# Linear attention stage: normalising on ScalarE, gates on GpSimd, shorter rank digits and softmax sum, and another order of the rounds

## The chip, the cores and the metric

One core of a Trainium2 chip runs the whole program. The time is that of one execution on the device in microseconds; three executions of the kernel before took 1861.42, 1862.78 and 1866.75 us (median 1862.78).

## The reference, cut to what matters

Sixteen sequences of 512 tokens of width 128 pass two layers. The change lies in the first: linear attention, a layer norm, and the routing of the mixture of experts that follows, with its shared expert.

```python
qkv = x @ W; q, k, v = split(qkv, 3)
q = elu(q) + 1; k = elu(k) + 1
KV = einsum('bld,blh->bhd', k, v); k_sum = k.sum(axis=1)
Z = 1 / (einsum('bld,bd->bl', q, k_sum) + 1e-6)
x = layernorm(x + einsum('bld,bhd,bl->blh', q, KV, Z))
probs = softmax(x @ gate_w.T)                # 32 experts
topk_w, topk_idx = top_k(probs, 4); topk_w /= sum(topk_w)
# the tokens of each expert in order of their number, 128 at most
# expert_out by its two matrices, gated, added; plus the shared expert
x = layernorm(x + routed + shared)
...
# second layer: state-space scan, layer norm, 8 experts with 2 of them, layer norm
```

## The kernel before, in words

Five engines run their own instruction lists and meet at semaphores: TensorE (PE) multiplies, VectorE (DVE), ScalarE (ACT) and GpSimd (POOL) compute, SyncE (SP) issues most DMAs. Up to about 270 us the program is in the first stage. It goes over the 16 sequences, one as a tile of 128 partitions by 4 times 128 columns. A sequence passes several steps, and each engine has a function `stage1` that in one round does the steps of several sequences in a fixed order: a is the newest sequence, r the one before it, l and p the two before that. TensorE's and VectorE's loops take two rounds in one turn; `at(per, k)` is the value of a semaphore that counts `per` to a sequence.

For sequence a: TensorE projects x to keys, values (kv, line 1091) and queries (q, line 1094). ScalarE takes the exponential, the copy of the values and the positive part (lines 863 to 870). VectorE adds them to kf and qf (lines 1467, 1475). TensorE makes the state kva (line 1125), ScalarE evicts it (kvx, line 885), TensorE multiplies by the queries (o, line 1131), VectorE divides and adds x (pre, line 1514) and takes the statistics. GpSimd makes 1/sqrt (rstd, lines 674, 676), and VectorE normalises (line 1452) into xg, whose last 32 columns take the gates.

For sequence r: TensorE transposes xg (line 1100), ScalarE evicts it (x1T, line 874), TensorE multiplies by the gate matrix and the shared expert's first matrices in one (line 1118). VectorE takes the eight largest logits of a row (top), subtracts the largest (lsub), finds the four chosen (mask, line 1500); ScalarE takes the exponential (lexp). VectorE multiplies both (gm, line 1509), sums (gs), inverts (gr) and writes the gates to xg (line 1529). The shared expert goes over hsh, its transpose (line 1137), its eviction (hshT, line 896) and the down product (line 1143) to resid. TensorE counts ranks from mask (lines 1147 to 1154), VectorE adds the carry of earlier sequences (rnk) and splits the rank into two digits by rounding with a large constant (rkt, rka, rkb, lines 1544 to 1551).

For sequence l: GpSimd subtracts the digits from all their values (dgb, dga, line 658), VectorE compares with zero (ohb, oha), ScalarE multiplies ohb by row and tile numbers (ohv, lines 889, 900). For sequence p: TensorE multiplies oha and ohv to a part of the experts' token lists (line 1110), and VectorE adds it to lsum (line 1471).

One order matters most: `need` is a wait until a tile has been read by its last user. So ohv of sequence l waits for the list product of the sequence before it, and TensorE's next projection writes into the memory that held o, so it waits for pre.

After the last round lsum is turned into indices (270 to 281 us), and the experts' tokens are gathered. SP's queue loads x two sequences ahead, and for each sequence stores a zero block, resid and xg, in that order, with a wait ahead of the last two.

## Time and profile before

| what | value |
| --- | --- |
| median of three runs | 1862.78 us |
| the profiled execution | 1860.44 us |
| its span, first to last instruction | 1858.8 us |
| mean granted TensorE clock over the span | 0.878 |
| TensorE, VectorE, ScalarE, GpSimd busy | 78%, 76%, 53%, 75% of the span |
| the first stage, to the end of the last lsum | 270.5 us |

The profiled execution is 1.6 us longer than its span, and 2.3 us shorter than the median. A row of the timeline has start, length, engine, line, operation, output and inputs with their shapes, and how many instructions were merged; in square brackets stands how long the engine was idle before it and what released it. A granted clock of 1.00 is 2.4 GHz, 0.50 is 1.2 GHz.

### The profile page before, as it was taken

What the parts mean: (1) busy time and instruction counts of PE and PEld (TensorE: products, weight loads), DVE (VectorE), ACT (ScalarE), POOL (GpSimd) and SP (SyncE); (2) the same over time, 40 slices, a digit from 0 to 9 for tenths busy, and PEclk for the clock granted to TensorE, in tenths of its full rate; (3) what the DMA queues carried; (4) which work ended last, traced back from release to release, by engine and by line L of the source; (5) the groups of instructions that cost most, each with busy time, mean ns of one, the idle gap of its engine ahead of it and who ended that gap; (6) DMA issues with size and microseconds to landing.
All of it is one profiled execution on the core that took longest, in us unless ns stands there. A gap on an engine that the chain in (4) does not pass through costs nothing.

```text
span 1858.8 us, 23733 instructions
## 1 busy us (share of the span) xinstructions
PE 1442.2 (78%) x5979; PEld 865.5 (47%) x6020; DVE 1407.2 (76%) x2764; ACT 977.2 (53%) x1676; POOL 1385.6 (75%) x962
## 2 busy tenths in 40 slices
PE   5777753425998889988899889988884989939881
PEld 3665642322443334433344334433342758938771
DVE  3898941112999999999999999999995576528884
ACT  2454520103655666556665566556642558827670
POOL 2554465753999999999999999999981455577785
PEclk8899965557999999999999899998997999969995
...
GB/s 149 110 89 89 103 161 218 63 45 128 68 105 91 126 131 75 93 96 129 131 58 85 120 131 103 75 88 163 120 7 127 36 65 129 149 82 158 149 147 81
DMA packets 201422, 198.62 MB, mean 107 GB/s; under 512 B 22664, under 2 KB 180296, under 8 KB 197064
## 3 DMA queue, kind: packets, MB, share of 16 engines
...
## 4 chain that ended last, share of the span: by engine, by line
PE 30%; DVE 21%; issue 15%; POOL 11%; DMA 6%; ACT 2%; DVEq 1%; POOLq 0%; SPq 0%; another core or an unknown queue 0%; ACTq 0%
PE bank L1272 12%; DVE hst L1646 11%; PE bank L1227 5%; POOL sorted_rows L828 3%; DMA sorted_rows<-x3b,row_of 2%; POOL yg L840 2%; DVE prod L1662 2%; POOL dbx L778 2%; PE bank L1261 1%; PE bank L1285 1%; PE bank L1225 1%; DVE st L1443 1%; PE bank L1239 1%; POOL xe L712 1%; DMA yg<-expert_rows,row_of 1%
## 5 line engine op out<-in xcount | busy, mean ns | idle before, releaser
L778 POOL TENSOR_TENSOR dbx<-u,ball 128x1024 f32<-128x1024 f32 x256 | 614.2, 2500 | 5.7 <-POOL u L809 2.8
L1646 DVE TENSOR_TENSOR_SCAN hst<-bank,dbx 128x512 f32<-128x512 f32 x512 | 592.3, 1207 | 8.6 <-POOL dbx L778 4.1
L1272 PE MATMUL bank<-prod,ident 128*128 128x512 f32 x1024 | 514.2, 639 | 20.1 <-DVE prod L1662 14.8
L983 ACT ACTIVATE bank<-dt,aneg 128x511 f32<-128x511 f32 x512 | 346.9, 689 | 276.9 <-DVE hst L1646 275.1
L1272 PEld LDWEIGHTS bank<-prod,ident 128*128 128x128 f32 x1024 | 207.1, 205 | 261.1 <-issue 210.8
L1662 DVE TENSOR_TENSOR prod<-hst,bank 128x1024 f32<-128x1024 f32 x192 | 233.7, 1217 | 17.2 <-DVE hst L1646 13.8
L787 POOL TENSOR_TENSOR prod<-hst,call 128x1024 f32<-128x1024 f32 x64 | 161.1, 2517 | 22.5 <-DVE hst L1646 22.3
L840 POOL DMA_INDIRECT yg<-expert_rows,row_of x128 | 128.6, 1005 | 47.2 <-issue 37.8
L1256 PE MATMUL bank<-parts,sel_c 128*128 128x512 bf16 x152 | 60.8, 401 | 73.6 <-DVE prod L1662 72.9
L828 POOL DMA_INDIRECT sorted_rows<-x3b,row_of x80 | 78.9, 986 | 51.6 <-DMA sorted_rows<-x3b,row_of 32.4
L1227 PE MATMUL bank<-x2T,inc 128*128 128x512 f32 x256 | 117.0, 600 | 0.0
L828 POOL DMA_INDIRECT sorted_rows<-x3a,row_of x48 | 46.8, 975 | 64.2 <-DMA sorted_rows<-x3a,row_of 36.5
L1365 PE MATMUL bank<-xu,wv 128*128 128x256 f32 x192 | 51.5, 391 | 42.1 <-DVE hg L1685 42.1
L1388 PE MATMUL bank<-wv,hg 128*128 128x128 f32 x384 | 77.0, 283 | 4.9 <-ACT yu L1058 4.9
L1256 PEld LDWEIGHTS bank<-parts,sel_c 128*128 128x128 bf16 x192 | 18.8, 98 | 132.3 <-DVE prod L1662 88.3
L1227 PEld LDWEIGHTS bank<-x2T,inc 128*128 128x128 f32 x256 | 49.4, 193 | 63.1 <-issue 63.1
L1052 ACT ACTIVATE hg<-hg 128x512 f32<-128x512 f32 x64 | 40.4, 632 | 67.8 <-DVE hg L1685 66.9
L1685 DVE SCALAR_TENSOR_TENSOR hg<-bank,wv,ha 128x256 f32<-128x256 f32 x96 | 42.0, 480 | 44.4 <-ACT ha L1036 44.0
L1389 PE MATMUL bank<-wv,hgb 128*128 128x128 f32 x384 | 75.5, 279 | 0.0
L1388 PEld LDWEIGHTS bank<-wv,hg 128*128 128x128 f32 x384 | 62.3, 196 | 12.0 <-ACT yu L1058 10.1
L658 POOL TENSOR_TENSOR dga<-rka,iota_e 128x2048 bf16<-128x2048 f32 x16 | 58.7, 3669 | 11.9 <-DVE ohb L1480 11.2
L658 POOL TENSOR_TENSOR dgb<-rkb,iota_e 128x1024 bf16<-128x1024 f32 x16 | 31.3, 1955 | 48.2 <-DVE rkb L1551 48.2
...
## 6 DMA issues: line engine op xcount, KB each, us to landing
...
```

Of the source, the lines that this page charges most:

```text
L658: gp.tensor_tensor(dst[:, :, :], a, b, ALU.subtract).then_inc(done, 1)
L778: gp.tensor_tensor(dbx[n % NDB][:, :, :], u[s.par][:, :, :], ball[:, n:n + 1, :].to_broadcast([P, NH, SEQ]), ALU.mult).then_inc(dbx_rdy, 1)
L787: gp.tensor_tensor(prod[2][:, :, :], hst[2][:, :, :], call[:, k:k + 1, :].to_broadcast([P, NH, SEQ]), ALU.mult).then_inc(pprod_rdy, 1)
L828: gp.indirect_dma_start(xs_d[b][:, :], bass.IndirectOffsetOnAxis(row_of[:, c, k:k + 1], 0), x3_tile(k), None).then_inc(sent[b], 16)
L840: gp.indirect_dma_start(yg[q % 3][:, k, c, :], None, y_d[b][:, :], bass.IndirectOffsetOnAxis(row_of[:, c, q * TT + k:q * TT + k + 1], 0)). ...
L983: act.activation(da_ps[h][:, 1:SEQ], dt_[s.par][:, h, 1:SEQ], ACT.Exp, scale=aneg[:, h, n:n + 1]).then_inc(da_rdy, 1)
L1227: last = mm(pb_ps[:, :], inc[:, k, tile(h)], x2T[:, k:k + SEQ], start=False, stop=(k == DCONV - 1))
L1256: mm(cb_ps[k % 2][:, :], sel_c[:, n, :], parts[s.par][:, :], start=True, stop=True).then_inc(cb_rdy, 1)
L1272: last = mm(y_ps[:, h, :], ident[:, :], from_[:, h, :], start=False, stop=(n == NS - 1), skip_group_check=True)
L1388: mm(yu_ps[:, tile(k)], hg[g % 2][:, tile(k)], w[:, W2A:W2B], start=True, stop=False)
L1646: dve.tensor_tensor_scan(h_of[:, h, :], da_ps[h][:, :], dbx[n % NDB][:, h, :], 0.0, ALU.mult, ALU.add).then_inc(scan_rdy, 1)
L1662: tt(prod[k % 2][:, :, :], h_of[:, :, :], over_h(cb_ps[k % 2]), ALU.mult).then_inc(prod_rdy, 1)
```

## The change

Five things change in the first stage; the rest of the program is as before, except that two semaphores are shared and so counted on.

- ScalarE normalises (one `activation` with scale rstd and bias -mean x rstd, four times a sequence). GpSimd makes the bias with two small instructions more.
- GpSimd multiplies lexp by mask and by gr and writes the gates.
- The sum of the softmax is that of the four largest: VectorE subtracts in `top` (tsub), ScalarE takes the exponential (texp), and the sum goes over four columns.
- The rank is split by one rounding with another constant (rka, rkb). The digits' values lie in two small tables.
- A round has six sequences: n (the next to be projected), a, r, l, p and o, whose lists are added. TensorE projects n, and ScalarE evicts it, in the middle of the round of a. All engines and SP's queue have another order. VectorE does resid for l, one round later than before, and lsum for o, also a round later. SP stores the gates ahead of resid, and loads x one sequence further ahead.

The diff, cut to the orders and the moved work (the bookkeeping lines `settle` and blank lines are left out without a mark):

```diff
...
+MAGIC_8 = 100663296.0
+MIDDLE = SLOT_B / 2 - 0.5
...
+def rounds(eng, stage, last):
+    q = lambda b: Seq(0, b) if 0 <= b < NB else None
+    for i in range(4):
+        stage(q(i), q(i - 1), q(i - 2), q(i - 3), q(i - 4), q(i + 1))
+    with eng.bass.Fori(0, NB // 2 - 3, engines=(eng.engine,), hint_back_edge=True) as j:
+        for i in (4, 5):
+            stage(*[Seq(j, i - k) for k in range(5)], Seq(j, i + 1))
+    for i in range(NB - 2, last):
+        stage(q(i), q(i - 1), q(i - 2), q(i - 3), q(i - 4), q(i + 1))
...
             def store_routed(s):
                 sp.dma_start(r2_d[bass.ds(s.at(SEQ), SEQ), :].rearrange("(t p) d -> p t d", p=P),
                              zero[:, 0:D].rearrange("p (t d) -> p t d", t=1).to_broadcast([P, TT, D])).then_inc(zeros_stored, 16)
+                sp.wait_ge(x1_rdy, s.at(TT, TT))
+                sp.wait_ge(gates_rdy, s.at(2, 2))
+                sp.dma_start(xg_d[bass.ds(s.at(SEQ), SEQ), :].rearrange("(t p) d -> p t d", p=P), xg[s.par][:, :, :]
+                             ).then_inc(st_xg[s.par], 16)
                 sp.wait_ge(resid_rdy, s.at(1, 1))
                 sp.dma_start(r_d[bass.ds(s.at(SEQ), SEQ), :].rearrange("(t p) d -> p t d", p=P), resid[:, :, :]
                              ).then_inc(st_r, 16)
-                sp.wait_ge(route0, s.at(15, 15))
-                sp.dma_start(xg_d[bass.ds(s.at(SEQ), SEQ), :].rearrange("(t p) d -> p t d", p=P), xg[s.par][:, :, :]
-                             ).then_inc(st_xg[s.par], 16)
...
+            def root_and_shift(s):
+                gp.wait_ge(mv_rdy, s.at(8, 8))
+                need(gp, x1_rdy, s.at(TT))
+                gp.tensor_scalar(rstd[:, :], mv[:, :, 1], LN_EPS, None, ALU.add).then_inc(rstd_rdy, 1)
+                gp.tensor_scalar(nmean[:, :], mv[:, :, 0], -1.0, None, ALU.mult).then_inc(rstd_rdy, 1)
+                gp.wait_ge(rstd_rdy, s.at(4, 2))
+                gp.tensor_tensor(rstd[:, :], rstd[:, :], neghalf[:, :], ALU.pow).then_inc(rstd_rdy, 1)
+                gp.wait_ge(rstd_rdy, s.at(4, 3))
+                gp.tensor_tensor(nmean[:, :], nmean[:, :], rstd[:, :], ALU.mult).then_inc(rstd_rdy, 1)
+            def gates_of(s):
+                gp.wait_ge(route0, s.at(14, 12))
+                gp.wait_ge(lexp_rdy, s.at(1, 1))
+                gp.tensor_tensor(gm[:, :, :], lexp[:, :, :], mask[:, :, :], ALU.mult).then_inc(gates_rdy, 1)
+                gp.wait_ge(gates_rdy, s.at(2, 1))
+                gp.wait_ge(route0, s.at(14, 14))
+                need(gp, st_xg[s.par], s.half(16))
+                gp.tensor_tensor(xg[s.par][:, :, D:XGW], gm[:, :, :], gr[:, :].rearrange("p (t e) -> p t e", e=1).to_broadcast([P, TT, E0]),
+                                 ALU.mult).then_inc(gates_rdy, 1)
...
+            def stage1(a, r, l, p, o, n):
+                if l:
+                    slots_of(l)
+                if a:
+                    root_and_shift(a)
+                if r:
+                    gates_of(r)
+            rounds(gp, stage1, NB + 2)
...
+            def stage1(a, r, l, p, o, n):
                 if a:
+                    act.wait_ge(kva_mm, a.at(1, 1))
+                    need(act, o_mm, a.at(1))
+                    act.activation(kvx[:, :], kva_ps[:, 0:D + 1], ACT.Copy).then_inc(kvx_rdy, 1)
                 if r:
                     act.wait_ge(t_mm, r.at(1, 1))
                     need(act, gu_mm, r.at(1))
                     act.activation(x1T[:, :], t_ps[:, :], ACT.Copy).then_inc(x1T_rdy, 1)
                     act.wait_ge(gu_mm, r.at(1, 1))
+                    need(act, route0, r.at(14))
                     act.activation(lg[:, :, :], gu_ps[:, :, 0:E0], ACT.Copy
                                    ).then_inc(lg_rdy, 1)
                     need(act, sg_rdy, r.at(1))
                     act.activation(tg[:, :, :], gu_ps[:, :, E0:E0 + I0], ACT.Tanh).then_inc(tg_rdy, 1)
                 if l:
                     act.wait_ge(ohb_rdy, l.at(1, 1))
                     need(act, list_mm, l.at(1))
                     act.activation(ohv[0][:, :, :, :], ohb[:, :, :, :], ACT.Identity, scale=row_no[:, 0:1]).then_inc(ohv_rdy, 1)
                     for k in range(TT):
                         act.activation(ohv[1][:, k, :, :], ohb[:, k, :, :], ACT.Identity, scale=tile_no[:, bass.ds(l.at(TT, k), 1)]
                                        ).then_inc(ohv_rdy, 1)
+                if r:
+                    act.wait_ge(route0, r.at(14, 6))
+                    need(act, gates_rdy, r.at(2))
+                    act.activation(texp[:, :, :], tsub[:, :, :], ACT.Exp).then_inc(texp_rdy, 1)
+                    act.activation(lexp[:, :, :], lsub[:, :, :], ACT.Exp).then_inc(lexp_rdy, 1)
+                if n:
+                    keys(n)
+                if r:
+                    act.wait_ge(hshT_mm, r.at(1, 1))
+                    need(act, d_mm, r.at(1))
+                    act.activation(hshT[:, :], t_ps[0:I0, :], ACT.Copy).then_inc(hshT_rdy, 1)
+                if n:
+                    queries(n)
+                if a:
+                    act.wait_ge(rstd_rdy, a.at(4, 4))
+                    need(act, st_xg[a.par], a.half(16))
+                    need(act, t_mm, a.at(1, -1))
+                    need(act, resid_rdy, a.at(1, -1))
+                    for k in range(TT):
+                        act.activation(xg[a.par][:, k, 0:D], pre[:, k, :], ACT.Identity, bias=nmean[:, k:k + 1], scale=rstd[:, k:k + 1]
+                                       ).then_inc(x1_rdy, 1)
...
+            def project(n):
+                pe.wait_ge(ldx[n.par], n.half(32, 32))
+                need(pe, pre_rdy, n.at(TT))
...
+                last.then_inc(kv_mm, 1)
+                need(pe, qf_rdy, n.at(1))
+                mm(q_ps[:, :], wt["Wq"][:, :], xT[n.par][:, :], start=True, stop=True).then_inc(q_mm, 1)
+            def stage1(a, r, l, p, o, n):
                 if a:
+                    pe.wait_ge(kf_rdy, a.at(1, 1))
+                    pe.wait_ge(v_rdy, a.at(1, 1))
+                    need(pe, list_sum, a.at(1, -3))
...
+                    last.then_inc(kva_mm, 1)
                 if r:
                     pe.wait_ge(x1_rdy, r.at(TT, TT))
                     need(pe, hshT_rdy, r.at(1))
+                    need(pe, rank0, r.at(4, -2))
...
                     last.then_inc(t_mm, 1)
+                if a:
+                    pe.wait_ge(kvx_rdy, a.at(1, 1))
+                    pe.wait_ge(qf_rdy, a.at(1, 1))
...
+                    last.then_inc(o_mm, 1)
+                if r:
+                    pe.wait_ge(x1T_rdy, r.at(1, 1))
+                    need(pe, lg_rdy, r.at(1))
+                    need(pe, hsh_rdy, r.at(1))
...
+                    last.then_inc(gu_mm, 1)
                 if p:
                     pe.wait_ge(ohv_rdy, p.at(5, 5))
                     pe.wait_ge(oha_rdy, p.at(1, 1))
+                    need(pe, list_sum, p.at(1))
...
                     last.then_inc(list_mm, 1)
+                if n:
+                    project(n)
                 if r:
                     pe.wait_ge(hsh_rdy, r.at(1, 1))
...
                     last.then_inc(hshT_mm, 1)
                     pe.wait_ge(hshT_rdy, r.at(1, 1))
                     need(pe, resid_rdy, r.at(1))
...
                     last.then_inc(d_mm, 1)
+                    pe.wait_ge(route0, r.at(14, 12))
...
+            def stage1(a, r, l, p, o, n):
+                if o:
+                    dve.wait_ge(list_mm, o.at(1, 1))
...
+                    tt(lsum[:, :], lsum[:, :], list_ps, ALU.add).then_inc(list_sum, 1)
                 if a:
                     dve.wait_ge(ek_rdy, a.at(1, 1))
...
                     stt(kf[:, :, :], ek[:, :, :], 1.0, kv_ps[:, :, 0:D], ALU.min, ALU.add).then_inc(kf_rdy, 1)
                     dve.wait_ge(eq_rdy, a.at(1, 1))
...
                     stt(qf[:, :], eq[:, :], 1.0, q_ps[:, :], ALU.min, ALU.add).then_inc(qf_rdy, 1)
                 if l:
+                    dve.wait_ge(d_mm, l.at(1, 1))
...
+                    tt(resid[:, :, :], blk4(d_ps), xg[l.par][:, :, 0:D], ALU.add).then_inc(resid_rdy, 1)
+                if a:
+                    dve.wait_ge(o_mm, a.at(1, 1))
+                    ts(den[:, :], o_ps[:, :, D], Z_EPS, None, ALU.add).then_inc(rz_rdy, 1)
...
+                    dve.reciprocal(rz[:, :], den[:, :]).then_inc(rz_rdy, 1)
+                if l:
                     dve.wait_ge(dg_rdy, l.at(2, 1))
...
                     ts(ohb[:, :, :, :].rearrange("p t e b -> p (t e) b"), dgb[:, :, :], 0.0, None, ALU.is_equal).then_inc(ohb_rdy, 1)
+                if a:
...
+                    dve.wait_ge(ldx[a.par], a.half(32, 32))
...
+                    for k in range(TT):
+                        stt(pre[:, k, :], o_ps[:, k, 0:D], rz[:, k:k + 1], xt[a.par][:, k, :], ALU.mult, ALU.add
+                            ).then_inc(pre_rdy, 1)
+                    dve.wait_ge(pre_rdy, a.at(TT, TT))
...
+                    stats_of(pre, stats, mv, a, mv_rdy)
                 if r:
                     dve.wait_ge(lg_rdy, r.at(1, 1))
...
                     dve.wait_ge(tg_rdy, r.at(1, 1))
...
                     tt(lsub[:, :, :], gu_ps[:, :, 0:E0], top[:, :, 0:1].to_broadcast([P, TT, E0]), ALU.subtract).then_inc(route0, 1)
...
+                    tt(tsub[:, :, :], top[:, :, 0:TOPK], top[:, :, 0:1].to_broadcast([P, TT, TOPK]), ALU.subtract).then_inc(route0, 1)
...
                     stt(sg[:, :, :], tg[:, :, :], 1.0, gu_ps[:, :, E0:E0 + I0], ALU.add, ALU.mult).then_inc(sg_rdy, 1)
                     dve.wait_ge(sg_rdy, r.at(1, 1))
...
                     tt(hsh[:, :, :], sg[:, :, :], gu_ps[:, :, E0 + I0:GW], ALU.mult).then_inc(hsh_rdy, 1)
...
                     tt(mask[:, :, :], rep[:, :, :], lg[:, :, :], ALU.not_equal).then_inc(route0, 1)
+                    dve.wait_ge(texp_rdy, r.at(1, 1))
+                    dve.tensor_reduce(gs[:, :], texp[:, :, :], AX.X, ALU.add).then_inc(route0, 1)
...
+                    dve.reciprocal(gr[:, :], gs[:, :]).then_inc(route0, 1)
                 if l:
                     dve.wait_ge(dg_rdy, l.at(2, 2))
...
                     ts(oha[:, :, :, :].rearrange("p t e a -> p (t e) a"), dga[:, :, :], 0.0, None, ALU.is_equal).then_inc(oha_rdy, 1)
                 if r:
                     dve.wait_ge(mt_mm, r.at(1, 1))
                     tt(rnk[:, :].rearrange("p (t e) -> p t e", t=TT), rank_ps.rearrange("p (t e) -> p t e", t=TT),
                        carry[:, :].rearrange("p (t e) -> p t e", t=1).to_broadcast([P, TT, E0]), ALU.add).then_inc(rank0, 1)
...
                     tt(carry[:, :], carry[:, :], tot_ps, ALU.add).then_inc(rank0, 1)
...
+                    ts(rka[:, :], rnk[:, :], MAGIC_8, MAGIC_8, ALU.add, ALU.subtract).then_inc(rank0, 1)
...
+                    tt(rkb[:, :], rnk[:, :], rka[:, :], ALU.subtract).then_inc(rank0, 1)
+            rounds(dve, stage1, NB + 4)
...
```

## Rows read from the trace of the kernel before

**Rows 1.** Busy time by stretch: length, each engine's busy us, granted clock, DMA share

```profile
60.39:231.64 171.25, 132.75 (x1135) 106.48 (x1131) 152.31 (x613) 88.86 (x193) 85.59 (x48) 0.91 0.33 96
231.64:270.46 38.82, 19.06 (x204) 17.32 (x200) 20.42 (x87) 12.09 (x27) 23.98 (x21) 0.63 0.47 137
```

**Rows 2.** Timeline, VectorE: kf of five sequences, the last lsum (start us, length us)

```profile
33.36 0.69 DVE L1467 SCALAR_TENSOR_TENSOR kf<-ek,bank 128x512 f32<-128x512 f32 x1 [8.90 <-ACT bank L866]
...
60.39 0.69 DVE L1467 SCALAR_TENSOR_TENSOR kf<-ek,bank 128x512 f32<-128x512 f32 x1
...
203.50 0.69 DVE L1467 SCALAR_TENSOR_TENSOR kf<-ek,bank 128x512 f32<-128x512 f32 x1 [0.33 <-issue]
...
217.37 0.68 DVE L1467 SCALAR_TENSOR_TENSOR kf<-ek,bank 128x512 f32<-128x512 f32 x1
...
231.64 0.69 DVE L1467 SCALAR_TENSOR_TENSOR kf<-ek,bank 128x512 f32<-128x512 f32 x1
...
270.04 0.42 DVE L1471 TENSOR_TENSOR lsum<-lsum,bank 128x256 f32<-128x256 f32 x1 [5.27 <-issue]
```

**Rows 3.** Instructions by line, VectorE, 100 to 214 us (busy us, mean ns)

```profile
L1452 DVE TENSOR_SCALAR xg<-pre,mv,rstd 128x128 f32<-128x128 f32 x32 | 8.9, 344 | 0.1
...
L1529 DVE TENSOR_TENSOR xg<-gm,gr 128x128 f32<-128x128 f32 x8 | 2.3, 291 | 0.3
...
L1546 DVE TENSOR_SCALAR rkt<-rkt 128x128 f32<-128x128 f32 x8 | 1.8, 227 | 0.3
```

**Rows 4.** Timeline: mask without and with GpSimd's dga; GpSimd's power

```profile
39.21 0.29 DVE L1500 TENSOR_TENSOR mask<-rep,lg 128x128 bf16<-128x128 f32 x1
...
120.63 3.67 POOL L658 TENSOR_TENSOR dga<-rka,iota_e 128x2048 bf16<-128x2048 f32 x1 [0.74 <-DVE ohb L1480]
...
122.76 1.68 DVE L1500 TENSOR_TENSOR mask<-rep,lg 128x128 bf16<-128x128 f32 x1
...
128.25 1.04 POOL L676 TENSOR_TENSOR rstd<-rstd,neghalf 128x4 f32<-128x4 f32 x1
```

**Rows 5.** Timeline, TensorE, one round at granted clock 1.00

```profile
217.08 1.10 PE L1110 MATMUL bank<-ohv,oha 128*128 128x64 bf16 x32
218.32 1.35 PE L1118 MATMUL bank<-wcat,x1T 128*128 128x160 f32 x8
219.51 1.06 PE L1125 MATMUL bank<-vext,kf 128*128 128x129 f32 x8
220.94 1.16 PE L1131 MATMUL bank<-kvx,qf 128*128 128x129 f32 x8 [0.37 <-ACT kvx L885]
...
223.25 1.16 PE L1143 MATMUL bank<-w_sd,hshT 64*128 64x128 f32 x8 [0.68 <-ACT hshT L896]
...
224.62 0.25 PE L1154 MATMUL bank<-mask,onesb 128*128 128x32 bf16 x4
```

**Rows 6.** Timeline, ScalarE: evictions, ohv and, from the second layer, x3o

```profile
115.35 0.60 ACT L863 ACTIVATE ek<-bank 128x512 f32<-128x512 f32 x1 [4.70 <-PE bank L1091]
...
116.84 0.60 ACT L869 ACTIVATE eq<-bank 128x512 f32<-128x512 f32 x1
...
120.95 1.14 ACT L889 ACTIVATE ohv<-ohb,row_no 128x1024 bf16<-128x1024 bf16 x1
...
122.86 0.59 ACT L896 ACTIVATE hshT<-bank 64x512 f32<-64x512 f32 x1 [0.57 <-PE bank L1137]
...
123.36 1.70 ACT L900 ACTIVATE ohv<-ohb,tile_no 128x256 bf16<-128x256 bf16 x4
...
541.74 1.50 ACT L1007 ACTIVATE x3o<-bank,nm,rs 128x128 f32<-128x128 f32 x4
```

**Rows 7.** Busy time of a stretch at low granted clock (columns as in rows 1)

```profile
47.50:50.50 3.00, 3.00 (x14) 2.83 (x12) 1.47 (x9) 0.55 (x2) 2.36 (x2) 0.50 0.73 230
```

**Rows 8.** Timeline, TensorE: kva in that stretch; a projection behind a wait

```profile
48.71 1.93 PE L1125 MATMUL bank<-vext,kf 128*128 128x129 f32 x8
...
111.83 3.48 PE L1091 MATMUL bank<-w_Wkv,xT 128*128 128x256 f32 x8 [1.08 <-DVE pre L1514]
```

252 lines of the change are left out of this document (80 added, 172 removed).

## The prediction

> **What bounds the kernel now.** I read the busy table by stretch first, then the timeline of two rounds, then durations by line, and last the rows where TensorE's granted clock is low. The change touches only the first stage (linear attention and its router, from the start to about 270 us of the 1858.8 us span); what follows starts from the finished lists and moves with their end. The stage works in rounds, one sequence entering per round. In the twelve rounds between the second and the last kf shown [rows 1, 2], 60.39 to 231.64 us, a round takes 171.25 / 12 = 14.27 us, and VectorE is busy for 152.31 / 12 = 12.7 us of it, TensorE 11.1, ScalarE 7.4, GpSimd 7.1. So VectorE bounds the round. The rounds shown whole take 13.87 us (203.50 to 217.37) and 14.27 us (to 231.64) [rows 2]. The last sequence then needs 38.8 us more, from its kf to the end of the last lsum [rows 1, 2].
>
> **What VectorE loses.** Per round go: the four normalising instructions (8.9 us in eight rounds, 1.11 each round), the two gate products (0.29 each), and two of the four steps that split the rank (0.23 each) [rows 3]: 2.1 us. The softmax sum over four columns instead of 32 gives at most 0.1 and needs a small subtraction more, bounded by 0 and by a product's 0.29; I take 0.2. A larger gain is hidden: mask takes 0.29 us where GpSimd is idle, and 1.68 us where GpSimd's dga runs; it starts at 122.76 and ends at 124.44, just after dga (120.63 + 3.67 = 124.30) [rows 4]. In the new order dga starts earlier against mask and is over by then, so 1.4 us more go. VectorE keeps 12.7 - 2.1 + 0.1 - 1.4 = 9.3 us of work a round. If it still bounded the round, 3.4 us would go from each.
>
> **What the new order chains together.** That gain is not on the path any more, because in the new order one chain goes through all engines once a round. I follow it from the start of kf at 0, with durations at the full clock. On TensorE the order is now kva, transpose of x1, o, gate/up product, list product, projection of the next sequence, hsh transpose, down product, ranks. kf ends at 0.69 and kva starts at 0.75 (1.06 long). The old gap from kva's start to o's start is 220.94 - 219.51 = 1.43 us and holds ScalarE's eviction; the transpose now sits in it and makes it about 1.5, so o starts at 2.3. o (1.16), gate/up (1.35) and list (1.10), less the 0.1 to 0.16 by which neighbours overlap (gate/up starts at 218.32 and kva at 219.51), end at 5.6 [rows 5]. ScalarE's ohv of sequence l may only overwrite its tile when the list product of sequence l-1 has read it; that product was early in the round and is now behind gate/up, so ohv starts at 5.7. The two steps of ohv take 1.14 + 1.70, 2.64 with their overlap, and the two exponentials behind them 0.3 (an estimate from the ratio of sizes to the 0.60 rows): 8.6. Only then come the three evictions of the next projection (115.35 to 116.84: 1.49), at 10.1, and the hsh eviction (0.59), at 10.7 [rows 6]. The down product waits for that and ranks stand behind it: 223.25 to 224.87, 1.62 us [rows 5], so 12.4. On VectorE the rank sum, carry, the two digits and the lsum of the next round, five instructions of 0.2 to 0.4 us [rows 2, 3], add 1.4 before the next kf. The sum is 13.8 us a round at the full clock, about what the shorter of the two rounds shown takes now. The projection itself (pre ends at 5.3, list at 5.6; by columns at kva's rate it is an estimated 3.1 us, so until 8.7) stands beside ohv, and the queries' two evictions and the normalising stand behind hsh's eviction, beside the down product.
>
> **Moved work costed at nothing, and its cover.** Normalising on ScalarE is like four of x3o, 1.50 us [rows 6]; it ends near 13.2, and the transpose that reads it comes at 15.3 in this count, so 2 us of cover; beyond that TensorE is held one for one. The gate products on GpSimd lie between dga / 16 = 0.23 us by size and the 0.6 of a full eviction; I take 0.5 each, since a fixed part must be there. GpSimd then carries dga (3.67), dgb (half of it, 1.8), the power (1.04), three small steps that I bound together by another 1.04, and the products, 8.6 us of 13.8 [rows 4]; its last product ends near 11.2 and the next digits come at 13.1. The stores and loads on SP's queue number the same; the gate store now goes ahead of the residual store and waits for a product of the round before, and the load of the next x stands in front of it: one round of cover each, cost 0, bounds 0 and 0.4 us a round.
>
> **The clock.** Between 47.5 and 50.5 us the granted clock was 0.50 (1.2 GHz) [rows 7], and kva took 1.93 us instead of 1.06 [rows 5, 8]. The projection at 111.83, after TensorE had waited 1.08 us for pre, took 3.48 us [rows 8]. Over the twelve rounds the clock averages 0.91 [rows 1], so TensorE is at the lower level for 18% of the time; today it can fall on the projection, as at 111.83, which has VectorE's work of 12.7 us a round beside it. In the new order TensorE waits twice: 1.5 us between hsh's transpose (an estimated 0.6 behind the projection, so 9.3) and the down product (10.8), and 2.1 us between the ranks (12.4) and the next kva (14.5), with 1.6 us of work between. The low stretches should therefore fall on kva, o, gate/up and list, which are all on the path. I price it so: the low share can hardly be under today's 18% of some 14.5 us, 2.6 us a round, of which five sixths meet TensorE work on the path and lose half: 1.1 us. With twice that share it is 2.2; with none it is 0. I take 1.1, since the waits are longer than today's but the work between is the same. A round is then 13.8 + 1.1 = 14.9 us.
>
> **The sum.** Twelve rounds: 12 x (14.9 - 14.27) = +7.6 us. The two rounds before them (33.36 to 60.39 [rows 2]) lack ohv or lists in either order: 0, bounds -1 and +1. The tail gains since VectorE's freed work and mask stand on its chain, but its clock is low for long (0.63 [rows 1]): -1.5 us, bounds -3 and 0. Together +6.1 us. The profiled execution took 1860.4 us, so 1866.5; the median of the runs, 1862.8, lies 2.3 above it, so I say **1869 us**.
>
> **Rivals.**
> First, **the clock holds** and the round is 13.8 us: 12 x (13.8 - 14.27) - 1.5 to -3 = -7.1 to -8.6 us, so 1855 us. The place is TensorE's wait between ranks and kva. It ends on the other side where low stretches cost under 0.6 us a round (13.8 + 0.6 = 14.4, and 12 x 0.13 pays for the tail). For it: TensorE's work from kva to the projection is now one unbroken stretch. Against it: the two long waits.
> Second, **both cancel**: low stretches in about half of the rounds, 14.1 to 14.7 us a round, which is -3.5 to +3.7 us: 1863.
> Third, **low in twice the share**: 2.2 us, a round of 16.0, 12 x 1.73 - 1.5 = +19 us: 1882. TensorE has then fallen to 1.2 GHz at the waits of every round, and recovers only behind gate/up. The Trainium skill (TensorE: Matmul & The Clock Gate, "What's actually happening") calls the throttled state the default that activity releases; by that rule the new waits bring this case, and the row at 111.83 agrees with its direction, though not every wait of today is followed by a low clock.
> Fourth, **VectorE's time is the round's time** after all, that is, the chain above is looser than I read it: 12 x -3.4 = -41 us, 1822. Against it: every link is an order on one engine or a tile that must be free.
>
> **How the numbers follow.** About 0.3% (5.6 us) is what a measurement of this kernel can tell from no change. The forecast has 0.36 (its own range 1866 to 1875), of which 0.04 would still measure within the bound, the third rival 0.07: slower 0.39. Both cancelling has 0.31, with those 0.04: same 0.35. The clock holding has 0.23 and the fourth 0.03: faster 0.26. The range from 1853 to 1880 leaves out the fourth, the far half of the third and the ends of the unknown costs.
>
> **What would show it.** In the changed kernel's profile kf should follow kf by 14.4 to 15.4 us; VectorE should wait for o (near 1.3 us) and, before the rank sum, for TensorE (near 0.5 to 1.5 us), and its busy time in the stage should fall by some 50 us without the stage ending earlier. Mask should take 0.3 to 0.5 us. ScalarE should run from the gate logits to hsh's eviction with hardly a gap, and ohv should start on the list product's end. Low-clock stretches should begin near the ranks and cover kva and o. I am wrong if kf follows kf by under 14 us, if the down product does not wait for ScalarE, or if the clock stays full at the start of the rounds.

## The result, and the profile after

The changed kernel takes **1891.79 us** (median of 4 runs, 1886.23 to 1893.11) against 1864.49 us (4 runs of the kernel before, on the same chip): a ratio of **1.0142, 95% interval 1.0115 to 1.0168**. It is slower by 27 us. Forecast were 1869 us and a range of 1853 to 1880: the sign is the forecast's, the size is not.

First, busy time by stretch in the changed kernel, with the columns of [rows 1] (length; busy us and count of TensorE, its weight loads, VectorE, ScalarE and GpSimd; granted clock, DMA share, GB/s): the twelve rounds from kf of the fourth sequence to kf of the last, the tail behind them, and two neighbouring stretches inside the rounds.

```profile
62.51:260.02 197.51, 146.98 (x1128) 127.97 (x1128) 120.97 (x529) 107.95 (x252) 102.30 (x97) 0.76 0.27 82
260.02:298.50 38.48, 21.82 (x216) 19.62 (x216) 19.47 (x78) 14.25 (x33) 23.78 (x26) 0.63 0.35 100
107.91:118.15 10.24, 7.71 (x45) 7.38 (x44) 4.01 (x12) 3.03 (x8) 2.16 (x2) 0.50 0.19 58
118.15:124.98 6.83, 5.00 (x52) 3.69 (x51) 6.12 (x33) 5.76 (x14) 6.15 (x6) 1.00 0.36 115
```

A round takes 197.51 / 12 = **16.46 us** where it took 14.27. VectorE is busy for 120.97 / 12 = 10.1 us of it, where it was 12.7, so it no longer bounds anything. The granted clock averages 0.76 where it was 0.91. In the middle of the stage three fifths of a round run at 1.2 GHz: 10.24 us at 0.50, then 6.83 us at 1.00.

The same rounds on VectorE's timeline (rows as in [rows 2]):

```profile
34.95 0.69 DVE L1519 SCALAR_TENSOR_TENSOR kf<-ek,bank 128x512 f32<-128x512 f32 x1 [13.10 <-ACT bank L916]
...
62.51 0.68 DVE L1519 SCALAR_TENSOR_TENSOR kf<-ek,bank 128x512 f32<-128x512 f32 x1
...
128.66 0.68 DVE L1519 SCALAR_TENSOR_TENSOR kf<-ek,bank 128x512 f32<-128x512 f32 x1
...
260.02 0.68 DVE L1519 SCALAR_TENSOR_TENSOR kf<-ek,bank 128x512 f32<-128x512 f32 x1
...
298.08 0.42 DVE L1515 TENSOR_TENSOR lsum<-lsum,bank 128x256 f32<-128x256 f32 x1 [2.05 <-PE bank L1194]
```

The stage ends at 298.50 us, 28.0 later than before (270.46). Of that, 1.6 us are there at the second kf (34.95 against 33.36), 0.5 come in the next two rounds (27.56 us against 27.03), 12 x 2.19 = 26.3 in the twelve rounds, and the tail gives 0.3 back (38.48 against 38.82). What follows the stage took 4.7 us more in this execution (1891.5 - 298.5 = 1593.0 against 1588.3). Its code is nearly the same; in the fifteen experiments below it took 1591 to 1601, so I read nothing from it.

One round of the chain, from the timeline of all engines:

```profile
112.52 2.08 PE L1164 MATMUL bank<-vext,kf 128*128 128x129 f32 x8 [2.53 <-DVE kf L1519]
...
115.25 1.93 PE L1177 MATMUL bank<-kvx,qf 128*128 128x129 f32 x8
...
116.97 1.83 PE L1184 MATMUL bank<-wcat,x1T 128*128 128x160 f32 x8
...
118.21 3.67 POOL L683 TENSOR_TENSOR dga<-rka,iota_a 128x2048 bf16<-128x2048 f32 x1 [4.99 <-DVE ohb L1535]
...
118.64 1.10 PE L1194 MATMUL bank<-ohv,oha 128*128 128x64 bf16 x32
...
119.77 1.15 ACT L942 ACTIVATE ohv<-ohb,row_no 128x1024 bf16<-128x1024 bf16 x1 [0.29 <-PE bank L1194]
...
121.11 0.81 DVE L1556 TENSOR_TENSOR tsub<-top 128x16 f32<-128x16 f32 x1
...
122.73 0.57 ACT L913 ACTIVATE ek<-bank 128x512 f32<-128x512 f32 x1
...
124.20 0.58 ACT L958 ACTIVATE hshT<-bank 64x512 f32<-64x512 f32 x1
...
124.83 1.97 PE L1208 MATMUL bank<-w_sd,hshT 64*128 64x128 f32 x8 [1.38 <-ACT hshT L958]
...
127.13 0.27 PE L1219 MATMUL bank<-mask,onesb 128*128 128x32 bf16 x4
...
127.44 0.29 DVE L1580 TENSOR_TENSOR rnk<-bank,carry 128x128 f32<-128x128 f32 x1 [2.76 <-PE bank L1219]
...
128.66 0.68 DVE L1519 SCALAR_TENSOR_TENSOR kf<-ek,bank 128x512 f32<-128x512 f32 x1
...
129.40 1.87 PE L1164 MATMUL bank<-vext,kf 128*128 128x129 f32 x7 [2.00 <-DVE kf L1519]
```

(The last row counts only the products inside the window.) Every link of the predicted chain is there, in its order: ohv starts 0.03 us after the list product's end, the keys' evictions and hsh's eviction stand behind it on ScalarE, the down product waits for the latter, the ranks stand behind that, and kva waits 2 us for kf. What differs is TensorE's own part: down, kva, o and gate/up take 1.97, 2.08, 1.93 and 1.83 us here, and took 1.16, 1.06, 1.16 and 1.35 in [rows 5].

Instructions by line from 62.51 to 260.02 us, answering to [rows 3, 4] (us busy, mean ns, idle us in front in all twelve rounds):

```profile
L967 ACT ACTIVATE xg<-pre,nmean,rstd 128x128 f32<-128x128 f32 x48 | 19.7, 490 | 0.0
...
L1208 PE MATMUL bank<-w_sd,hshT 64*128 64x128 f32 x96 | 17.9, 342 | 15.5 <-ACT hshT L958 15.5
...
L1556 DVE TENSOR_TENSOR tsub<-top 128x16 f32<-128x16 f32 x12 | 10.0, 835 | 0.0
L713 POOL TENSOR_TENSOR gm<-lexp,mask 128x128 f32<-128x128 f32 x12 | 9.1, 755 | 0.7
...
L718 POOL TENSOR_TENSOR xg<-gm,gr 128x128 f32<-128x128 f32 x12 | 4.8, 401 | 3.7 <-POOL gm L713 3.7
...
L1569 DVE TENSOR_TENSOR mask<-rep,lg 128x128 bf16<-128x128 f32 x12 | 3.5, 292 | 1.3
...
L1529 DVE TENSOR_SCALAR den<-bank 128x4 f32<-128x4 f32 x12 | 1.9, 162 | 42.3 <-PE bank L1177 42.3
```

The mask takes 0.29 us in every round, as said. VectorE waits 42.3 / 12 = 3.5 us a round for o. GpSimd's exclusion has moved to tsub, which has 16 elements a partition and takes 0.84 us.

### The profile page after: what moved, and what is told of

Its sections match the earlier page's. It is cut to its first block, busy times and chain, and to the rows that moved or that the text cites. A ratio compares the mean times of both kernels' runs of the same rounds, so it can differ in the third digit from the quotient of the medians.

```text
span 1891.5 us, 23767 instructions
## 1 busy us (share of the span) xinstructions
PE 1458.5 (77%) x5979; PEld 890.3 (47%) x6020; DVE 1368.0 (72%) x2652; ACT 1001.0 (53%) x1756; POOL 1406.8 (74%) x1028
## 4 chain that ended last, share of the span: by engine, by line
PE 28%; DVE 19%; issue 15%; POOL 12%; DMA 8%; ACT 1%; DVEq 1%; POOLq 0%; SPq 0%; another core or an unknown queue 0%; ACTq 0%
PE bank L1329 13%; DVE hst L1673 11%; PE bank L1284 5%; POOL sorted_rows L879 5%; POOL yg L891 3%; DMA sorted_rows<-x3a,row_of 3%; DMA sorted_rows<-x3b,row_of 2%; DVE prod L1689 2%; PE bank L1318 1%; PE bank L1282 1%; PE bank L1342 1%; PE bank L1296 1%; DVE st L1500 1%; POOL dbx L829 1%; DVE y L1659 1%
## 5 line engine op out<-in xcount | busy, mean ns | idle before, releaser
L1689 DVE TENSOR_TENSOR prod<-hst,bank 128x1024 f32<-128x1024 f32 x192 | 233.4, 1216 | 17.2 <-DVE hst L1673 13.8
L683 POOL TENSOR_TENSOR dga<-rka,iota_a 128x2048 bf16<-128x2048 f32 x16 | 58.7, 3672 | 64.3 <-issue 36.1
L771 POOL DMA_INDIRECT resid_rows<-ye,ixs x32 | 50.8, 1587 | 19.3 <-issue 13.6
```

What stands on the lines that cost most here:

```text
L1689: tt(prod[k % 2][:, :, :], h_of[:, :, :], over_h(cb_ps[k % 2]), ALU.mult).then_inc(prod_rdy, 1)
```

## Experiments

The ratios are to the kernel before, measured on the same chip as each kernel; the changed kernel's own is 1.0142. "A round" is the mean of the twelve from the fourth kf to the last in the profile.

### Is it the clock? Three kernels with TensorE kept at work

The edit of **e1_fill**: small products of constants into the gate/up bank, in both waits. Behind hsh nobody reads that bank until the next gate/up product.

```diff
+            def fill(n):
+                for k in range(n):
+                    mm(gu_ps[:, k % TT, 0:P], onesb[:, :], upper[:, :], start=True, stop=True)
...
                     last.then_inc(hshT_mm, 1)
+                    fill(20)
                     pe.wait_ge(hshT_rdy, r.at(1, 1))
...
                     last.then_inc(mt_mm, 1)
+                    fill(28)
```

> The changed kernel with TensorE kept at work in its two long waits: 20 small bf16 products (128 columns, 0.055 us each at the full clock by the ranks' rows) ahead of the down product, 28 behind the ranks, into the gate/up bank, which nobody reads by then; no output changes. Theory, the clock: the chain alone is 13.8 us a round and the low clock makes it 16.5, so with the clock held kf should follow kf by 13.8 to 14.4 us and the time fall by 12 x 2.1 to 2.7 = 25 to 32 us, to 1860 to 1867. Rival, the chain is longer than summed and the low clock only falls into time that is waited anyway: kf to kf stays above 16 and the time above 1885; where the fillers delay kva and the down product, it is slower than the changed kernel by up to 12 x 1.5 = 18 us.

Measured: 1865.7 us, ratio 0.9990 [0.9966, 1.0014]: the whole loss is gone. Busy time of its twelve rounds, and TensorE's timeline at the start of one:

```profile
60.14:228.42 168.28, 148.44 (x1714) 128.16 (x1712) 121.01 (x529) 108.66 (x252) 102.39 (x97) 1.00 0.32 97
```

```profile
159.01 1.15 PE L1168 MATMUL bank<-vext,kf 128*128 128x129 f32 x8 [0.90 <-DVE kf L1525]
...
160.62 1.16 PE L1181 MATMUL bank<-kvx,qf 128*128 128x129 f32 x8
161.61 1.25 PE L1188 MATMUL bank<-wcat,x1T 128*128 128x160 f32 x8
...
169.11 1.16 PE L1213 MATMUL bank<-w_sd,hshT 64*128 64x128 f32 x8
```

The clock is 1.00 through all twelve rounds, and a round takes 168.28 / 12 = 14.02 us. VectorE, ScalarE and GpSimd are as busy as in the changed kernel to within 1 us; nothing but the clock and the 576 fillers is different. So the low clock costs 16.46 - 14.02 = **2.44 us a round**, 29 us in the stretch.

**e11_fill_down** keeps the first `fill(20)` alone.

> The changed kernel with the 20 fillers ahead of the down product alone, and none behind the ranks. If the wait ahead of the down product is what lets the clock fall, the round is e1_fill's 14.0 us and the time 1863 to 1869. If it is the wait between the ranks and kva, the round stays at 16 us or more, 1883 to 1892. If both do, half comes back: 14.6 to 15.6 us, 1872 to 1883.

Measured: 1872.3 us, ratio 1.0043 [1.0024, 1.0062], a round 180.07 / 12 = 15.01 us, clock 0.92. Both waits count: filling the one ahead of the down product brings back 1.45 us of the 2.44, and filling the one between the ranks and kva as well brings the other 1.0. The second wait was not filled alone.

```profile
59.03:239.10 180.07, 140.77 (x1368) 122.17 (x1368) 121.04 (x530) 108.25 (x252) 102.38 (x97) 0.92 0.30 91
```

**e8_before_fill** puts 10 and 16 fillers at the same places into the kernel *before*.

> The kernel before with filling products at the same two places, 10 ahead of the down product and 16 behind the ranks. Theory: there the low clock (0.91 on average) falls mostly beside VectorE's 12.7 us of work a round and costs little: 0 to 0.4 us a round back, 1858 to 1866 where the kernel before has 1863 to 1867. Rival: the low clock costs the old order as well, 0.18 x 14.27 / 2 = 1.3 us a round: 1847 to 1851. Rival, slower: the fillers delay the next projection, up to 12 x 0.9 us, 1876.

Measured: 1874.15 us, ratio 1.0028 [1.0013, 1.0042], which is 8 us above the range that the theory gave.

```profile
60.40:232.14 171.74, 139.51 (x1431) 117.66 (x1427) 152.56 (x613) 88.86 (x192) 85.57 (x48) 0.97 0.33 96
```

The rounds have the clock at 0.97 instead of 0.91 and take 171.74 / 12 = 14.31 us, against 14.27, and VectorE is as busy in them as before (152.56 us against 152.31). What the run loses lies behind them, 2.4 us of it in the tail (41.2 us against 38.8). So with two thirds of its low time gone the old order's round was no shorter: its low stretches lay beside VectorE's work. That is why the same clock could be overlooked there and not here.

### Is the chain the chain? One link shortened at a time

**e4_ranks_first** puts the ranks ahead of the down product, both behind hsh's eviction.

```diff
                     pe.wait_ge(hshT_rdy, r.at(1, 1))
-                    need(pe, resid_rdy, r.at(1))
...
-                    last.then_inc(d_mm, 1)
                     pe.wait_ge(route0, r.at(14, 12))
...
                     last.then_inc(mt_mm, 1)
+                    need(pe, resid_rdy, r.at(1))
...
+                    last.then_inc(d_mm, 1)
```

> The changed kernel with the ranks ahead of the down product on TensorE (both still behind ScalarE's eviction of hsh). Theory, one chain: the down product, 1.97 us at the low and 1.16 at the full clock, leaves the way to the rank sum and kf and lies beside VectorE's five small steps: 1.2 to 2.0 us off each of 12 rounds, 14 to 24 us, to 1868 to 1878. Rival, the clock sets the period: 1886 to 1892, with kf to kf near 17 us from 94 to 180 us. Rival, slower: the shorter wait in front of kva moves nothing and resid, later now, holds VectorE: above 1892.

Measured: 1872.32 us, ratio 1.0038 [1.0024, 1.0052], a round 178.14 / 12 = 14.84 us: 1.6 us off, the middle of what was expected.

```profile
59.55:237.69 178.14, 142.29 (x1129) 123.17 (x1128) 121.06 (x529) 108.50 (x254) 102.33 (x97) 0.81 0.30 92
```

The down product was on the path to kf because the ranks stood behind it. But the 1.6 us are not the link's alone: the clock rose from 0.76 to 0.81, which is 38% of 14.84 us or 5.6 us at the low level against 7.9, and at the 2.44 / 7.9 = 0.31 us that such a microsecond cost in the changed kernel that is an estimated 0.7 us.

**e3_ohb_early** puts ohb ahead of VectorE's wait for o.

```diff
                     tt(resid[:, :, :], blk4(d_ps), xg[l.par][:, :, 0:D], ALU.add).then_inc(resid_rdy, 1)
+                if l:
+                    dve.wait_ge(dg_rdy, l.at(2, 1))
+                    need(dve, ohv_rdy, l.at(5))
+                    ts(ohb[:, :, :, :].rearrange("p t e b -> p (t e) b"), dgb[:, :, :], 0.0, None, ALU.is_equal).then_inc(ohb_rdy, 1)
                 if a:
                     dve.wait_ge(o_mm, a.at(1, 1))
```

> The changed kernel with ohb (its digits are ready at 113.2) put ahead of the wait for o on VectorE, where that engine stands idle for 3.6 us. GpSimd's dga then ends before tsub. Theory, one chain: ohb's 0.43 us leaves the way from o to hsh, and tsub, 0.81 us now because it ends only with dga, shrinks to about 0.2: 1.0 us off each round, 12 to 13 us, to about 1879; TensorE's wait before the down product shrinks by at most the 0.6 us until ScalarE's ohv ends, and if ohv and the keys behind it hold that wait, only 0 to 0.5 us of each round is gained: 1886 to 1892. Rival, moved operations are what costs (the lock between GpSimd and VectorE): the gain is larger than 1.0 us a round, below 1875.

Measured: 1885.54 us, ratio 1.0101 [1.0073, 1.0130], a round 15.62 us: 0.8 us less, where 1.0 was expected, or at most 0.5 if ohv and the keys hold the wait.

```profile
63.16:250.60 187.44, 136.92 (x1128) 118.49 (x1128) 113.78 (x530) 107.52 (x252) 104.37 (x97) 0.82 0.28 86
```

```profile
L1208 PE MATMUL bank<-w_sd,hshT 64*128 64x128 f32 x96 | 13.9, 285 | 22.0 <-ACT hshT L958 22.0
```

ohv and the keys do hold it: the down product waits 22.0 us for ScalarE in the twelve rounds, and 15.5 in the changed kernel. What shortened the round is mostly the clock again, 0.82 against 0.76: by the estimate given for e4_ranks_first 0.7 of the 0.8 us. So ohb and tsub were hardly on the chain.

**e2_kf_first** makes kf and qf a function of their own, `features`, and calls it for the next sequence ahead of the rank sum.

```diff
+                if n:
+                    features(n)
                 if r:
                     dve.wait_ge(mt_mm, r.at(1, 1))
```

> The changed kernel with the next sequence's kf and qf put ahead of the rank sum on VectorE. Theory, one chain: rank sum, carry, two digits and lsum stand between the ranks and kf, from 127.44 to 128.66 us in the profile of the changed kernel, and kva starts 2.0 us after the ranks end; kf's input is there 3 us before. With kf ahead, kva follows the ranks at once: 2.0 us off each of some 13 rounds, 26 us, to about 1866, and more (to 1855) where the shorter wait also lifts the clock. Rival, VectorE's later work or the normalising is as late: kva then waits in front of the transposes and under 6 us are gained. Rival, the clock alone sets it: the period stays near 17 us in the stretch from 94 to 180 us and nothing is gained there.

Measured: 1884.91 us, ratio 1.0120 [1.0084, 1.0156], far above the 1866 expected. The next run shows the miss best. **e5_fill_kf** is e2_kf_first with 24 fillers ahead of the down product.

> The changed kernel with kf and qf ahead of the rank sum (as in e2_kf_first) and 24 filling products ahead of the down product; none behind the ranks, since that wait is gone with kf there. Theory, a chain whose length the clock sets: e2_kf_first ran its two rounds at the full clock in 11.94 and 11.99 us (43.50 to 67.43) and then, with low stretches, 15.5 on average; with the clock held all rounds should take 12.0 to 12.5: 12 x 2 us less than e1_fill's 14.02, that is 1840 to 1848, and below the kernel before. Rival, one filled wait is not enough: low stretches stay in every second round or more, 13.5 to 15 us a round, 1858 to 1876.

Measured: 1863.77 us, ratio 0.9975 [0.9961, 0.9990], a round 14.0 us, clock 0.96: in the range of the rival, and not the 1840 to 1848 expected. Rounds at the full clock take 13.3 to 13.8 us there. One row of its TensorE timeline tells what I had left out:

```profile
99.39 0.82 PE L1168 MATMUL bank<-vext,kf 128*128 128x129 f32 x5 [1.85 <-DVE lsum L1528]
```

kva (whose last products lie outside the window) waits 1.85 us, and no longer for kf but for lsum. kva and the list lie in one PSUM bank, and the kernel has kva wait until VectorE has added the list (`need(pe, list_sum, ...)`); lsum still stood behind the ranks. The two rounds of 12 us at the full clock, from which I took the expectation, had no list sum yet. A wait has two ends to move, and I moved one.

### The chain made shorter

**e6_list_early** joins e5_fill_kf and e3_ohb_early and moves the list product to the start of the round, ahead of kva, with its sum behind ScalarE's eviction of kva. **e10_no_fill** is the same without fillers.

```diff
             def stage1(a, r, l, p, o, n):
+                if p:
+                    pe.wait_ge(ohv_rdy, p.at(5, 5))
...
+                    last.then_inc(list_mm, 1)
                 if a:
                     pe.wait_ge(kf_rdy, a.at(1, 1))
...
-                if o:
-                    dve.wait_ge(list_mm, o.at(1, 1))
+                if p:
+                    dve.wait_ge(list_mm, p.at(1, 1))
+                    dve.wait_ge(kvx_rdy, a.at(1, 1) if a else NB)
```

> e5_fill_kf with two more steps taken off the chain: ohb ahead of the wait for o on VectorE (e3_ohb_early), and the list product moved from behind gate/up to the start of the round, ahead of kva, with the list sum behind ScalarE's eviction of kva. Theory: the list product's 1.1 us is on the chain at either place, but ScalarE's ohv may then start behind the tanh, 0.4 us earlier, and lsum's 0.42 leaves the chain, so 11.2 to 12.0 us a round: 1830 to 1842. Rival: the list product ahead of kva delays kva by its whole 1.1 us and ohv is held by something else: 12.5 to 13 us a round, 1846 to 1854. Rival, the clock falls in the longer wait between projection and hsh's transpose: above 1856.

Measured: 1847.29 us, ratio **0.9894** [0.9877, 0.9910], a round 149.27 / 12 = 12.44 us at clock 1.00. That is near the first rival's figures, and faster than both kernels.

> e6_list_early without any filling products. Theory, the wait ahead of the down product alone lets the clock fall: low stretches in most rounds, 13.5 to 15.5 us a round, 1860 to 1885. Rival, with the list product moved into the other wait TensorE stays busy enough: no or few low stretches, 12.1 to 12.6 us, 1844 to 1851. This tells whether the fillers or the shorter chain hold the clock in e6_list_early.

Measured: 1844.03 us, ratio 0.9898 [0.9874, 0.9923]. The rival was right. Its twelve rounds, and the seven of them between 105.83 and 190.11:

```profile
53.76:205.21 151.45, 121.66 (x1128) 99.84 (x1128) 115.24 (x530) 106.90 (x253) 103.75 (x97) 0.95 0.35 106
105.83:190.11 84.28, 67.52 (x659) 54.68 (x660) 66.66 (x310) 62.91 (x149) 60.54 (x57) 1.00 0.38 114
```

Those seven take 84.28 / 7 = 12.04 us each, at the full clock and without fillers. With the list product in the wait between ranks and kva these rounds need no filler. The waits in them are shorter than those of the changed kernel too (at most 1.2 us on TensorE from 118 to 145 us, against 2.5 in the row at 112.52), and which of the two holds the clock was not separated.

**e9_best** takes three more things off the chain: the list sum goes behind oha, hsh's eviction goes ahead of two of the keys' evictions, and there are 14 fillers instead of 24. **e13_short_chain** drops the fillers and puts rank sum, carry and digits between kf and qf.

```diff
                 if n:
-                    keys(n)
+                    keys_exp(n)
                 if r:
...
                     act.activation(hshT[:, :], t_ps[0:I0, :], ACT.Copy).then_inc(hshT_rdy, 1)
                 if n:
+                    keys(n)
+                if n:
                     queries(n)
```

> e6_list_early with three more steps: the list sum behind the one-hot oha and no longer between o and the row sums (0.41 us), ScalarE's eviction of hsh behind the first of the keys' three evictions and no longer behind all (hsh's transposes end at 165.75, the eviction starts at 166.15: 0.4 us), and 14 fillers in place of 24 (24 of them ended 0.3 us after the eviction). Theory, one chain at the full clock: 12.3 - 1.0 = 11.2 to 11.6 us a round, 8 to 13 us less than e6_list_early: 1834 to 1840. Rival, 14 fillers don't hold the clock: low stretches come back, 1847 or more. Rival, something else is next (the keys' evictions in front of kf, or GpSimd's dga in front of tsub): 12.0 us, 1842 to 1847.

Measured: 1838.89 us, ratio **0.9861** [0.9842, 0.9880], but 148.46 / 12 = 12.37 us a round, no shorter than e6_list_early. The stage ends 2.0 us earlier (244.8 us against 246.9); the rest of the 8 us between the medians lies behind it, and the intervals of the two ratios overlap. The next bound was one row away: ohb now waits for the digits, `[1.68 <-POOL dgb L683]`, and den, which could start at o's end (160.61), starts at 161.60.

> e9_best without fillers (e10_no_fill held the full clock without them in nine rounds) and with the rank sum, carry and the two digits between kf and qf on VectorE. In e9_best the digits were ready only at 158.97, so ohb waited 1.68 us for GpSimd's dgb and den started 1.0 us after o's end. Theory, that wait is the chain's: digits 1.0 us earlier, den on o's end: 12.4 - 0.7 to 1.0 = 11.4 to 11.7 us a round, 8 to 12 us less than e9_best: 1827 to 1832. Rival, qf, now 0.7 us later, holds o: 12.0 to 12.4 us, 1836 to 1842. Rival, without fillers the clock falls in some rounds, as in three of e10_no_fill's: +1 us in each, 1832 to 1845.

Measured: 1840.32 us, ratio 0.9867 [0.9845, 0.9890]: the same as e9_best. Five of its rounds:

```profile
129.35:186.66 57.31, 48.54 (x472) 39.30 (x471) 48.09 (x221) 44.75 (x106) 42.50 (x40) 1.00 0.39 120
```

57.31 / 5 = 11.46 us, as the chain said. But single rounds of 12.96 and 16.41 us with low stretches bring the mean of twelve to 12.03, and what the stage still gains (its end is at 240.1 us against 244.8) does not show in the medians.

### Order or operations? The changed operations in the old order

**e7_old_order** keeps before's order on every engine and has the four changed operations in it. On GpSimd and at the end of ScalarE's round, against the kernel before:

```diff
+            def stage1(a, r):
+                if a:
+                    root_and_shift(a)
+                if r:
+                    gates_of(r)
+                    slots_of(r)
...
+                if a:
+                    act.wait_ge(rstd_rdy, a.at(4, 4))
...
+                        act.activation(xg[a.par][:, k, 0:D], pre[:, k, :], ACT.Identity, bias=nmean[:, k:k + 1], scale=rstd[:, k:k + 1]
+                                       ).then_inc(x1_rdy, 1)
```

> The order of the kernel before on all engines, with the changed operations in it: normalising on ScalarE at the end of its round, both gate products on GpSimd ahead of the digits, the rank digits by one rounding, the softmax sum from the four maxima. Theory, the new order is what costs: VectorE, which bounds the old order, loses 2.1 us of work a round and the time falls by 12 x 1 to 2.1 us or more, to 1837 to 1853. Rival, the moved operations cost (GpSimd's products and root, ScalarE's normalising as late as before's): the round does not shorten, or lengthens; 1860 to 1892. By e1_fill the rival is the less likely.

Measured: 1910.1 us, ratio 1.0221 [1.0204, 1.0238], a round 16.87 us: slower than the changed kernel, and above the range of the rival too. Four rows of its timeline:

```profile
196.58 3.63 PE L1140 MATMUL bank<-w_Wkv,xT 128*128 128x256 f32 x8
...
199.63 1.65 ACT L949 ACTIVATE xg<-pre,nmean,rstd 128x128 f32<-128x128 f32 x4 [4.01 <-POOL nmean L691]
...
202.85 0.69 DVE L1508 SCALAR_TENSOR_TENSOR kf<-ek,bank 128x512 f32<-128x512 f32 x1 [3.93 <-ACT bank L905]
...
206.99 1.68 DVE L1532 TENSOR_TENSOR tsub<-top 128x16 f32<-128x16 f32 x1
```

VectorE waits 3.9 us for ScalarE ahead of kf (3.7 to 4.0 in all twelve rounds). The normalising waits for GpSimd's root and stands ahead of the keys' evictions there, and the projection of this round, nearly all of it at the low clock, takes 3.63 us (2.6 in the mean of the twelve). The cover that VectorE's work gave is gone in this order too.

In **e12_old_norm_dve** the normalising goes back to VectorE, behind the rank sum:

```diff
+                if a:
+                    need(dve, st_xg[a.par], a.half(16))
+                    need(dve, t_mm, a.at(1, -1))
+                    normalise(xg[a.par], pre, mv, rstd, a, rstd_rdy, x1_rdy)
```

> As e7_old_order (the order of before with the changed operations), but with the normalising left on VectorE at its old place; GpSimd has the gate products, ranks are split by one rounding, the softmax sum comes from the four maxima. Theory: in e7_old_order kf waited 3.9 us a round for ScalarE, where the normalising stands behind GpSimd's root and ahead of the keys' evictions; with it back on VectorE that wait is gone, and VectorE has 0.46 (digits) and 0.58 (gate products) less than before: 13.2 to 14.2 us a round, 1849 to 1863. Rival, the gate products on GpSimd delay root and digits (1.2 us of work ahead of dgb), or tsub's lock with dga (1.68 us in e7_old_order) eats the gain: 14.3 to 16 us, 1864 to 1885.

Measured: 1885.99 us, ratio 1.0116 [1.0095, 1.0138], a round 15.90 us. The wait ahead of kf falls from 3.8 to 1.0 us in the mean (0.2 to 1.6 in single rounds), but 1.6 us a round of loss stay.

In **e14_old_tsub_late** tsub stands behind hsh as well:

```diff
-                    tt(tsub[:, :, :], top[:, :, 0:TOPK], top[:, :, 0:1].to_broadcast([P, TT, TOPK]), ALU.subtract).then_inc(route0, 1)
...
                     tt(hsh[:, :, :], sg[:, :, :], gu_ps[:, :, E0 + I0:GW], ALU.mult).then_inc(hsh_rdy, 1)
+                    need(dve, texp_rdy, r.at(1))
+                    tt(tsub[:, :, :], top[:, :, 0:TOPK], top[:, :, 0:1].to_broadcast([P, TT, TOPK]), ALU.subtract).then_inc(route0, 1)
```

> e12_old_norm_dve with tsub, the subtraction that the softmax sum from the four maxima adds, behind hsh instead of ahead of it. In e12_old_norm_dve it took 2.2 us, since GpSimd's dga runs beside it, and stood ahead of sg and hsh; TensorE then waited 2.1 us for hsh, and its projection ran at the low clock (3.42 us). Theory, the subtraction's place is what makes the old order slower with the changed operations: hsh comes 2 us earlier, 13.8 to 14.6 us a round against 15.9, 1855 to 1868. Rival, the gate products ahead of the digits on GpSimd, or the exponentials that now wait for tsub, hold it all the same: 15 to 16 us, 1874 to 1887.

Measured: 1875.76 us, ratio 1.0057 [1.0035, 1.0080], a round 178.78 / 12 = 14.90 us. tsub's place is worth 1.0 us a round, less than the 1.3 to 2.1 expected. It still takes 1.46 us, and the exponential that needs it stands ahead of hsh's eviction on ScalarE. So TensorE's wait has only moved: in e12_old_norm_dve it was 22.5 / 12 = 1.9 us ahead of hsh's transposes and 0.7 ahead of the down product, here it is none and 24.0 / 12 = 2.0:

```profile
200.41 1.46 DVE L1515 TENSOR_TENSOR tsub<-top 128x16 f32<-128x16 f32 x1
...
202.94 1.59 PE L1171 MATMUL bank<-w_sd,hshT 64*128 64x128 f32 x8 [1.71 <-ACT hshT L924]
```

**e15_before_digits** is the kernel before with the one rounding alone:

```diff
                     need(dve, dg_rdy, r.at(2))
-                    ts(rka[:, :], rkt[:, :], MAGIC, None, ALU.subtract).then_inc(rank0, 1)
+                    ts(rka[:, :], rnk[:, :], MAGIC_8, MAGIC_8, ALU.add, ALU.subtract).then_inc(rank0, 1)
...
-                    stt(rkb[:, :], rka[:, :], -float(SLOT_B), rnk[:, :], ALU.mult, ALU.add).then_inc(rank0, 1)
+                    tt(rkb[:, :], rnk[:, :], rka[:, :], ALU.subtract).then_inc(rank0, 1)
```

> The kernel before with one part of the change alone: the rank split by one rounding, two VectorE instructions of 0.23 us fewer, at the same place, ahead of the next round's kf. Theory, VectorE's time is the old order's round: 12 x 0.46 = 5.5 us off, to 1857 to 1862 where the kernel before has 1862 to 1867 (ratio 0.997). Rival, the order's other waits take it: same within 2 us (ratio 0.999 to 1.001), with a wait of 0.4 to 0.5 us ahead of kf on VectorE.

Measured: 1860.79 us, ratio 0.9975 [0.9964, 0.9986], a round 13.96 us. Two instructions fewer in the place where VectorE is the bound are worth 0.3 us a round, two thirds of their length. The 0.6 us a round between e14's 14.90 and the 14.27 of before was not taken apart; the gate products on GpSimd were not run alone. Nor were these runs repeated with fillers, so how much of their loss is the clock's (0.82, 0.82 and 0.88 in e7, e12 and e14, against 0.91) is not shown.

## Why the prediction was wrong

**The step that failed** is the price of the low clock: "I take 1.1, since the waits are longer than today's but the work between is the same." It measured 2.44 us a round (changed kernel against e1_fill), above even the 2.2 that it gave for twice the share. 12 x (2.44 - 1.1) = 16 us of the 23 that the forecast was short of; the chain's 14.02 us for 13.8 (2.6), the start (1.6) and the tail (1.2) make most of the rest. The term was built as a share of time at 1.2 GHz times what that costs. The cost per low microsecond was priced too high, not too low (five sixths of a half, 0.42, against a measured 2.44 / 7.9 = 0.31). The share was wrong: I carried today's 18% over as a floor, and it became (1 - 0.76) / 0.5 = 48%, 7.9 us of 16.46. I also expected the low stretch to begin near the ranks. In the five rounds whose down products start from 107.59 to 176.1 us it began with the down product: at 124.83 the clock is still 1.00 (the stretch to 124.98), falls 0.15 us later, and the product takes 1.97 us, so one more link was at the lower level. In the other seven it began behind the down product (1.16 us), as expected; kva took about 2.1 us in all twelve. e11_fill_down shows that each of the two waits has its part.

That was the **third rival**: "TensorE has then fallen to 1.2 GHz at the waits of every round, and recovers only behind gate/up", a round of 16.0 us and 1882. Its mechanism is what the rows show: the clock is back at 118.15 us, before the end of gate/up (116.97 + 1.83). It had a chance of 0.07, and its price was still 10 us short. The Trainium skill (TensorE: Matmul & The Clock Gate, "What's actually happening"), which calls the throttled state the default that activity releases, points the same way; e1_fill agrees, since activity of no use to the result held 1.00 for 168 us.

**The chain was right.** 13.8 us were summed for the round at the full clock; e1_fill measured 14.02. In the round of e1_fill whose kf starts at 158.20, o, ohv, hsh's eviction and the next kf start 2.4, 5.6, 10.2 and 13.8 us after it; 2.3, 5.7, 10.1 and 13.8 were counted. The links and their order are also in the rows at 112.52 to 129.40, and with links taken off, rounds at the full clock get shorter: 13.3 to 13.8 us in e5_fill_kf, 12.04 in e10_no_fill, 11.46 in e13_short_chain. Not every step was worth its length: in e2_kf_first and e9_best the next wait (lsum, the digits) stood right behind.

**VectorE** kept 10.1 us of work a round, not 9.3 (in the whole stage 162.85 us instead of 201.33: 38 fewer, not 50). One step left short was the softmax sum: "needs a small subtraction more, bounded by 0 and by a product's 0.29". tsub takes 0.84 us, above that bound: dga locks it as it had locked the mask (1.68 us in [rows 4]). The Trainium skill (SBUF — State Buffer, "SBUF: two separate sides") states that a VectorE operation with two inputs from SBUF and a GpSimd operation that reads SBUF exclude each other for a whole instruction. The rows agree: tsub ends with dga here (121.92 and 121.88 us), and took 0.17 us in e3_ohb_early, where dga had ended 3 us before it came (115.84 and 119.05). I had priced the lock's going from mask and not asked which operation comes under it next. Off the path this costs little in the new order (e3_ohb_early), but its place was worth 1.0 us in the old one (e14, with the clock at 0.88 instead of 0.82). The other step was the mask itself: 1.68 us was one round's, and in the mean of the twelve rounds before it took 1.45, so 1.16 went and not 1.4:

```profile
L1500 DVE TENSOR_TENSOR mask<-rep,lg 128x128 bf16<-128x128 f32 x12 | 17.4, 1454 | 0.4
```

**The moved work** cost a little more than its prices: normalising 19.7 / 12 = 1.64 us against 1.50, the gate products 0.76 and 0.40 against 0.5 each, the first of them above its bound of 0.6. The cover held: in the rows shown of the changed kernel no other engine waits for one of them, and only the second gate product waits for the first (3.7 / 12 = 0.3 us). The first two rounds cost +0.5 us where 0 with bounds of -1 and +1 stood; the tail gave 0.3 us where 1.5 was taken, inside the bounds of 0 and 3. The start added 1.6 us that no term had.

**The first rival**, the clock holds, gave 1855 us; with the clock held by hand it was 1865.7, ratio 0.999. So even then the change gained nothing measurable: it takes 2.6 us a round from VectorE and spends them on a chain.
